# Two silus issued earlier on ScalarE, tile loads moved between steps, and the small tile's last product placed between two others

## The reference, cut to what matters

```
xn = layernorm(x)                                  # x: 4 x 1024 x 1024 fp32
s  = xn + attention over the batch axis (4 x 4 scores for each of 1024 positions)
Wg, Wu, Wd = NF4[codes] * scales of 64-blocks       # I = 2752, H = 1024
g  = silu( (silu(xn @ Wg.T) * (xn @ Wu.T)) @ Wd.T )
out = x + s * g
```

## Time and profile before

| what | value |
|---|---|
| median of 3 runs | 2513.22 us (2512.47 to 2515.49) |
| profiled execution, its own time | 2514.81 us |
| span in its profile | 2513.0 us |
| PE busy | 2414.7 us (96%), 11214 matmuls |
| DVE, ACT, POOL busy | 64%, 40%, 3% |
| mean granted TensorE clock | 0.985 |

### The profile page before, as it was taken

One profiled execution on the slowest core, in us unless ns is written; L12 is line 12 of the kernel. 1 busy time (PEld: TensorE's weight loads), 2 busy tenths in 40 slices (PEclk: granted clock), 3 DMA queues, 4 the chain that ended last, 5 costly groups with the idle time before them and its releaser, 6 DMA issues.

```text
span 2513.0 us, 30203 instructions
## 1 busy us (share of the span) xinstructions
PE 2414.7 (96%) x11214; PEld 1108.0 (44%) x11214; DVE 1604.2 (64%) x2751; ACT 1006.6 (40%) x1144; POOL 84.5 (3%) x72
## 2 busy tenths in 40 slices
PE   2889999999999989999999999999999999999999
PEld 1434444444444434444444444444444444444444
DVE  8888777668988857788877886656422432431431
ACT  8876777777778424444454521110000000000001
POOL 0000000000000000000000000000010011001011
PEclk7899999999999999999999999999999999999999
DMA  6856675657766795556655644229767766777764
GB/s 241 257 199 203 197 225 193 212 170 264 239 235 215 267 323 191 189 201 209 221 182 183 208 176 145 107 102 367 301 244 314 307 270 269 298 287 290 302 261 163
DMA packets 171854, 579.51 MB, mean 231 GB/s; under 512 B 17632, under 2 KB 42896, under 8 KB 153916
## 3 DMA queue, kind: packets, MB, share of 16 engines
q1 hardware_dynamic: 136716, 289.21, 33.9%
q10 hardware_dynamic: 34992, 288.37, 29.9%
HBM read 388.76 MB, written 188.75 MB: 230 GB/s over the span
## 4 chain that ended last, share of the span: by engine, by line
PE 87%; DVE 4%; issue 3%; DMA 3%; ACT 2%; SPq 0%; POOL 0%; ACTq 0%; POOLq 0%; DVEq 0%
PE ps L1764 55%; PE ps L1910 31%; DMA arena<-in_x 1%; ACT arena L760 1%; PE ps L1837 1%; PE ps L1721 1%; DMA arena<-xnsc 1%; DMA arena<-in_dn 1%; DVE arena L1291 0%; ACT arena L773 0%; DVE arena L1380 0%; DMA arena<-in_gu 0%; DVE arena L1223 0%; DVE arena L1433 0%; DVE arena L1312 0%
## 5 line engine op out<-in xcount | busy, mean ns | idle before, releaser
L1764 PE MATMUL ps<-arena 128*128 128x512 f16 x7152 | 1562.8, 381 | 34.5 <-ACT arena L966 11.3
L1764 PEld LDWEIGHTS ps<-arena 128*128 128x128 f16 x7152 | 701.7, 98 | 883.0 <-issue 19.4
L1910 PE MATMUL ps<-arena 128*128 128x512 f16 x3696 | 797.9, 379 | 0.3 <-issue 0.3
L760 ACT ACTIVATE arena<-arena,bias_t 128x2048 f32<-128x2048 f32 (+3 forms) x288 | 525.0, 1829 | 86.6 <-DMA arena<-in_dn 77.5
L1910 PEld LDWEIGHTS ps<-arena 128*128 128x128 f16 x3696 | 361.6, 98 | 436.6 <-issue 0.8
L1380 DVE TENSOR_TENSOR arena<-arena 128x512 f16<-128x512 f32 x364 | 243.1, 683 | 9.8 <-ACT arena L918 8.5
L1178 ACT ACTIVATE arena<-arena,e_d 128x512 f32<-128x512 f32 x48 | 34.6, 721 | 424.3 <-DVE arena L1686 219.4
L966 ACT ACTIVATE arena<-ps,gate_back 128x512 f32<-128x512 f32 x84 | 57.2, 681 | 301.7 <-PE ps L1764 301.5
L729 POOL TENSOR_TENSOR arena<-arena 128x512 f32<-128x512 f32 x64 | 82.5, 1297 | 2414.5 <-DMA arena<-in_xt 2106.1
L976 ACT ACTIVATE arena<-arena,gate_back 128x512 f32<-128x512 f32 x84 | 60.5, 720 | 179.1 <-DVE arena L1550 166.2
L1662 DVE SCALAR_TENSOR_TENSOR arena<-arena,sc 128x512 f32<-128x512 f32 x192 | 129.8, 743 | 0.0
(11 more groups left out here) (109 smaller groups left out, 1158.1 us busy)
## 6 DMA issues: line engine op xcount, KB each, us to landing
isc<-arena SPq DMA_DIRECT2D x308, 256.0 KB, 2.4
arena<-wdsc ACTq DMA_DIRECT2D x28, 2816.0 KB, 10.1
arena<-isc ACTq DMA_DIRECT2D x28, 2816.0 KB, 18.0
arena<-xnsc SPq DMA_DIRECT2D x48, 1024.0 KB, 8.5
wsc<-arena ACTq DMA_DIRECT2D x21, 1792.0 KB, 6.9
arena<-in_x SPq DMA_DIRECT2D x48, 512.0 KB, 6.0
arena<-in_gu ACTq DMA_DIRECT2D x43, 512.0 KB, 4.6
wdsc<-arena SPq DMA_DIRECT2D x77, 256.0 KB, 2.1
```

The costliest lines, as they stand in the source:

```text
L760: a_.activation(buf, src, ACT.Prelu, bias=bias_t[:, i:i + 1], scale=scale, alpha=alpha).then_inc(ramps, 1)
L1764: ins = t_.matmul(ps[:, bank, :], wreg[:, b, w, wa, k, :], xreg[:, j, o, k, xa, :], start=start and (k, wa, xa) == (0, 0, 0), stop=stop an ...
L1910: ins = t_.matmul(ps[:, bank, :], ring_w[b][:, k, wa, g, :], ring_i[b][:, k, xa, :], start=first and (k, wa, xa) == (0, 0, 0), stop=r not ...
```

## The change

1. `sil_a(s-1)` now stands in front of `w_high(2, 6)` in step 3.
2. In step 4 all ramps of tile 4 (`ramps_of(s, 0, 4)`) come behind `sil_a(3)` instead of partly in front, and `load_codes(4)` is issued in step 4, behind the high parts of tile 3, instead of at the end of step 3.
3. Behind a step of the rest, `halves` gives p1, p6 (of s), then p2 of the rest's step, then p7, p5. `second_half` of that step moves on DVE to a place between q and v of step s. This concerns steps 42, 44 and 86.
4. The rest's weights lie in slots 4 and 1 (`REST_W`) instead of 0 and 1: two 512-column high and low parts instead of one of 1024, a strided store, and other slots in the reload of the second half. At the turn slot 0 of tile 0 is loaded with slots 5 and 6 in step 41, and slot 4, which only p5 of step 44 reads, is loaded in step 43 with a semaphore of its own, `w4_in`.
5. The codes of tile 23 are loaded in step 42 instead of step 44.

```
-    if s > 2:
-        out += half(s - 1, SECOND, SECOND_REST)
-    return out
+    behind = half(s - 1, SECOND, SECOND_REST) if s > 2 else []
+    if out and STEPS[s - 1][1] == LAST:
+        return out[:2] + behind + out[2:]
+    return out + behind
...
+                for o, to in enumerate(REST_W):
+                    ins = a_.activation(wflat[:, b, to, 0, :], yb[2 * (LAST % 2)][:, 512 * o:512 * o + 512], ACT.Copy)
+                ins.then_inc(w_hi, 1)
...
                     act.wait_ge(prod, prod_at(39, "p3"))
-                    load_w(0, 4, 7)
+                    load_w(0, 0, 1)
+                    load_w(0, 5, 7)
...
-                if s in DOWN_AT and DOWN_AT[s][1] == 0 and DOWN_AT[s][0] + 1 < NDOWN:
+                if s in DOWN_AT and DOWN_AT[s][1] == 0 and 0 < DOWN_AT[s][0] < NDOWN - 1:
                     load_codes(NU + DOWN_AT[s][0] + 1)
+                if s == 42:
+                    load_codes(NU + 1)
...
+                if s == 4:
+                    load_codes(4)
...
-                if late:
+                if late and s != 4:
                     ramps_of(s, 2, 3)
+                if s > 2:
+                    sil_a(s - 1)
                 if s == 3:
                     w_high(2, 6)
-                if s > 2:
-                    sil_a(s - 1)
...
                     act.wait_ge(prod, prod_at(43, "r"))
-                    load_w(0, 0, 1)
+                    act.dma_start(wflat[:, wbuf(1, 0), 4, :, :], wsc[0, :, 4, :, :]).then_inc(w4_in, 16)
...
-                ramps_of(s, 3 if late else 2, 4)
+                ramps_of(s, 0 if s == 4 else 3 if late else 2, 4)
...
                 v_.tensor_tensor(q, ps[:, p6_bank(s), :], p1sb, ALU.add).then_inc(q_made, 1)
                 background(s, 1)
+                if s > 2 and STEPS[s - 1][1] == LAST:
+                    second_half(s - 1)
...
-                        pe.wait_ge(w_in[b][1 if w in (1, 2, 3) else 0], 32 * loads - (16 if u == LAST else 0))
+                        if u == 0 and w == REST_W[0]:
+                            pe.wait_ge(w4_in, 16)
+                        else:
+                            pe.wait_ge(w_in[b][1 if w in (1, 2, 3) else 0], 32 * loads - (16 if u == LAST else 0))
```

More of the change, by code:

```diff
@@ L42 @@
 FIRST_REST, SECOND_REST = ["p1", "r"], ["p2"]
+REST_W = [4, 1]
 DOWN_ORDER = ["p1", "p6", "p2", "p7", "p5", "p4", "p3"]
@@ L386, in build @@
         xb_in = [[sem(f"xb_in{j}{o}") for o in range(7)] for j in (0, 1)]
+        w4_in = sem("w4_in")
         prod = sem("prod")
@@ L778, in w_high_last @@
                 act.wait_ge(wst[LAST % 2], 16 * (LAST // 2))
+                act.wait_ge(prod, prod_at(step_of(0, LAST - 2, 1), "p5"))
                 act.wait_ge(prod, prod_at(step_of(0, LAST - 2, 1), "p2"))
-                a_.activation(wflat[:, b, 0:2, 0, :], yb[2 * (LAST % 2)].rearrange("p (o c) -> p o c", o=2), ACT.Copy).then_inc(w_hi, 1)
+                for o, to in enumerate(REST_W):
+                    ins = a_.activation(wflat[:, b, to, 0, :], yb[2 * (LAST % 2)][:, 512 * o:512 * o + 512], ACT.Copy)
+                ins.then_inc(w_hi, 1)
             def store_w(u):
@@ L785, in store_w @@
                 if u == LAST:
-                    act.dma_start(wsc[u, :, 0:2, :, :], wflat[:, b, 0:2, :, :]).then_inc(wst[u % 2], 16)
+                    act.dma_start(wsc[u, :, 1:5:3, :, :], wflat[:, b, 1:5:3, :, :]).then_inc(wst[u % 2], 16)
                 else:
@@ L1126, in _ @@
                     act.wait_ge(prod, prod_at(43, "r"))
-                    load_w(0, 0, 1)
+                    act.dma_start(wflat[:, wbuf(1, 0), 4, :, :], wsc[0, :, 4, :, :]).then_inc(w4_in, 16)
                 elif s == NSTEP + 40:
-                    load_w(LAST, 0, 1)
+                    load_w(LAST, 4, 5)
                     load_w(LAST, 1, 2)
@@ L1139, in _ @@
                     c_high(job, 3)
-                if 3 <= s < 40 and j:
+                if 4 <= s < 40 and j:
                     load_codes(u + 3)
@@ L1277, in w_item @@
                         dve.wait_ge(w_hi, w_base(u, 7, 1) + 1)
-                        v_.tensor_tensor(wflat[:, b, 0:2, 1, :], tg.rearrange("p (o c) -> p o c", o=2), wflat[:, b, 0:2, 0, :],
-                                         ALU.subtract).then_inc(w_lo, 1)
+                        for o, to in enumerate(REST_W):
+                            ins = v_.tensor_tensor(wflat[:, b, to, 1, :], tg[:, 512 * o:512 * o + 512], wflat[:, b, to, 0, :], ALU.subtract)
+                        ins.then_inc(w_lo, 1)
                     return
@@ L1641, in _ @@
                     background(s, 4)
-                if s > 2:
+                if s > 2 and (s == TOTAL or STEPS[s - 1][1] != LAST):
                     second_half(s - 1)
@@ L1859, in _ @@
                     if u == LAST and name == "r":
[L1860 to L1863, removed]
+                        for k, (w, o) in enumerate(zip(REST_W, (4, 2))):
+                            need(t, name, w, o)
+                            ins = product(t, bank, w, o, k == 0, k == 1)
                     else:
-                        w, o = (OPERAND[name],) * 2 if u != LAST else (0, 0) if name == "p1" else (1, 1)
+                        w, o = (OPERAND[name],) * 2 if u != LAST else (REST_W[0], 0) if name == "p1" else (REST_W[1], 1)
                         need(t, name, w, o)
```

## The result

| | before | after |
|---|---|---|
| median | 2514.26 us (4 runs, 2512.47 to 2515.49) | 2499.01 us (4 runs, 2497.79 to 2499.58) |
| ratio, 95% interval | | 0.9942 [0.9928, 0.9956] |
| profiled execution: own time, span | 2514.81, 2513.0 us | 2499.58, 2497.8 us |
| PE busy | 2414.7 us | 2409.7 us |

The account below looks back on a forecast made before the run. PE, busy 2414.7 of 2513.0 us, was taken as the bound, with its breaks. The terms 2.5 + 3.3 + 3.6 + 9.9 - 2.5 = 16.8 us took the median 2513.2 to 2496.4, stated as 2496.5, range 2490 to 2503.

Parts of the forecast that it names:

- Part 1: Silus of steps 3 and 4 on ACT moved forward: 2.5 us gained, bounds 0 to 5, limited by DVE.
- The item on the slow start near 276: PE behind 276.35: half of the 1.6 us of slow matmuls there was counted as saved.
- The last item: Ramps of tile 4: their codes, issued later, land after 9 us and cost 0.3 us.
- Rival (a): Steps 4 and 5: both silu breaks saved in full, 13.4 us instead of 2.5, time 2485.5 us; chance 0.07.
- rival (d): Step 3: late codes of tile 4 delay DVE, kernel slower; breaks even at 26 us of landing; chance 0.02.
- Part 2: Steps 43 and 87: PE's two 1.65 us waits for silu and multiplication go, 3.3 us.
- Part 3: Step 44: PE's 3.57 us break at 905.7, for the load of slot 0, goes, 3.6 us.
- Part 4: Turn, codes of tile 23 loaded earlier: PE's losses of 7.17 and 2.7 us go, 9.9 us.
- The deduction: Step 44: slot 1 of tile 0 lands 2 to 4 us late; 2.5 us off the gain, ends 0 and 6.
- The second path: Step 46, p7: scale rows of tile 22, about 14.6 us to land, may delay DVE; would overlap with slot 1's delay.
- Rival (b): Turn held by its transfers: costs over 6 of the 9.9 us, gain 6 to 10, 2503 to 2507 us; chance 0.14.
- rival (c): Slots 4 and 1 land so late that the turn takes as long; within 0.2%, 2508 us and up; chance 0.05.

Follow-up runs that it names:

- no_silus: The changed kernel with steps 3 and 4 on ACT put back as before; 2501.19 us, ratio 0.9954 to the kernel before.
- silus_only: The kernel before with only the silus, ramps and tile 4 codes of steps 3 and 4 moved; 2510.26 us, ratio 0.9988.
- codes4_old_place: The changed kernel with the codes of tile 4 asked for at the end of step 3 again; 2500.37 us, ratio 0.9952 to the kernel before.
- slots_only: The kernel before with only the rest's weights in slots 4 and 1 and slot 0 of tile 0 loaded in step 41; 2513.15 us, ratio 0.9994.
- slot1_first: The changed kernel with slot 1 of tile 0 asked for in front of two token operands; 2495.2 us, ratio 0.9924 to the kernel before.
- slot1_scales: As slot1_first, with the scale rows of tile 22 asked for in step 42 instead of 43; 2493.70 us, ratio 0.9915 to the kernel before.

## Why the prediction was right, point by point

**Part 1** was forecast as 2.5 us with 0 to 5. The mechanism is shown: PE stands for DVE's addition of p4 in steps 4 and 5 (forecast 3.1 and about 5; seen 2.22 and 2.92, and 3.10 and 4.12 in the run of part 1 alone), then for the silu of step 7, 3.8 us earlier than before. It measured 3.0 us alone and 3.0 in the change, by ratios that are uncertain by more than 2 us. At the mark of the short wait (354.03 before, 350.9 to 354.5 in the four other kernels without part 1 whose token tiles are all loaded; 347.7 to 349.8 in the six with it) the traces give some 4 us. The term was a little small: DVE could follow further than the 1.6 us that I read from its wait for PE at 203.02 (there is a second one, of 0.36 us at 192.66). The addition of p3 that waited there runs at 199.00 now, 4.0 us earlier. Part of it is that DVE's token tile came 1.9 us earlier (177.43 against 179.30); in the seven traces with the codes' old place and all token tiles it came at 178.5 to 179.8, in the four with the new place at 177.2 to 178.2, so the later codes, which I had down as a loss of 0.3, seem to have made room for it. The item on the slow start near 276 came out in full and not by half: the break there shrank from 2.47 to 0.79 us and nothing slow stands behind it, while the silu's break at 255.56 has one now (7.04 us for 24 matmuls against 5.35). Some of the 5.5 us at the mark is chance: `no_silus` has it 3.1 us earlier than the kernel before, and nothing that was changed between the two bears on PE before step 40. The last item, codes landing 9 us after they are asked for, was near: they are asked for at 168.62 and used at 176.86, and no cost of theirs can be told, as their old place shows. Rival (a), both breaks in full, and rival (d), the codes, are out by `silus_only` and `codes4_old_place`.

**Part 2**, 3.3 us: the waits are gone, and 3.8 us were measured alone (1.5 to 6.0). **Part 3**, 3.6 us: its break is gone in the change, but by these runs the term can hold only together with part 4: alone it gave 1.5 us by the ratio, which cannot be told from nothing. I added the terms without saying that. **Part 4**, 9.9 us: 9.6 by the ratio alone, 7.4 by the medians, and 8.2 in its trace, since 1.61 us of the break goes only with part 2. The four parts alone sum to 17.9 us by the ratios and the change gives 14.6; by the medians it is 15.3 and 15.3, so whether the parts simply add up stays open.

**The deduction** of 2.5 us, with 0 and 6 as ends, is the term that was mis-sized. The path was named rightly: slot 1 was the last of a row of loads, and it was 4.19 us late, with some 1.5 us lost to the lower level behind it (19.44 us for the first 83 matmuls against 83 x 0.216 = 17.9), 5.7 in all. The slow start was left out, though the same kind of loss stood in the other terms. The wait was 1.7 us longer than the 2.5. The times behind it were both wrong, and nearly cancelled. Slot 1 landed at 925.85, not at 929 to 931 (my own steps, 929.2 plus 3.6 less up to 3, give 929.8 to 932.8). PE came for it at 921.7, not at 927.6, a figure that left part 1's lead out. PE was earlier by its lead at the mark, and the landing moved with it, since that load waits for a product of PE (see `no_silus`). The bytes were counted at 359 GB/s, and while slot 1 was in flight the engines moved 6.17 MB in 18.6 us, 332 GB/s; I estimate 1.4 us from these two rates for that stretch. The second path, the scale rows, was named too, and is shown by `slot1_first` (2.74 us once the first path is free) and `slot1_scales` (both free, 6.8 us gained by the ratio).

**The sum.** The deduction was 3.2 us too small (5.7 against 2.5), and the whole forecast was 2.5 us too low, so the other terms together came to 0.7 us more than forecast. That they came so near is in part luck. By the two profiled executions the lead was 5.5 us at the mark (2.5 forecast, and partly chance), 9.4 at the turn (15.1 us of breaks and slow starts before, 5.7 after) and 1.65 in step 87; some 2.4 were lost near 1105 and 1326, where nothing was forecast.

**Rivals.** Rival (b), over 6 us lost at the turn, was only just missed, and its two halves do not fit: a loss of 6 us would give a gain of 13.3, 2499.9, and not the 6 to 10 us that it names, for which 9 or more must be lost; rival (c), no change because slots 4 and 1 both land late, is out, since slot 4 held nothing in the change.

**What stays open.** PE's waits for DVE near 1105 and 1326 took 3.1 us in the trace after and 2.3 in that of before, and a slow start of 1.7 us stands behind the first of them. In the other traces they sum to between 1.4 and 3.7 us, with and without the change; I take them for chance, and no run isolates them.

**The scale rows' time to landing.** The Trainium skill, DMA: Bandwidth & Descriptors, section Queues, rings and completion order, says that each DMA engine goes round the queues that have work, a packet at a time. From this the prediction had worked out, for an equal split in bytes, some 6 us for the scale rows on SP's queue; they landed after 17.1 (median of four). While they were asked for, 901.8 to 904.4, the two queues moved (packets, MB, share of the time of 16 engines; q10 is ACT's, q1 SP's):

```profile
q10 hardware_dynamic: 205, 0.60, 59.2%
q1 hardware_dynamic: 227, 0.42, 41.5%
```

The numbers of packets are near each other and the bytes are not, so this stretch agrees with packets taken in turn, and it was the step from packets to bytes that failed. SP's queue also carried stores that had been issued before the scale rows. How much of the 17.1 us was theirs no run shows.

## What to carry to other kernels

When waits follow one another in front of the same transfers, cost them as a chain. Taking away the first alone moved its time into the next in `slots_only`; in the changed kernel, where the load that the last wait hung on is moved up as well, both breaks are gone. Where a stage becomes shorter, sum up the bytes that must land in it and look at which load is asked for last; its place in the queue can be worth more than the moment at which it is asked for (`slot1_first`: 0.13 us earlier, 2 MB less in front, landed 5.5 us earlier). And where an in-order engine has a ramp or a high part in front of a silu that the bound engine waits for, moving it gains only up to what the next engine can follow.

## What the runs showed of the hardware that had not been expected

Whether a slow start follows a break does not go by the break's length alone. In step 4 PE stood for 3.10 us in `silus_only` and did the next 84 matmuls in 18.30 us, at a granted clock of 1.00 from the start; in the changed kernel it stood for 2.22 us and took 19.99, with 0.66 in the first 5 us; in `slots_only` it stood for 3.29 and took 21.18, with 0.50 in the first 5 us. In the kernel before, 3.57 us cost nothing more and 2.47 us cost 1.6. So in these traces breaks between 2 and 3.6 us cost their length and from 0 to 2.9 us more. This kernel has about five breaks of that kind, and that may be a good part of the spread between executions of one kernel (2509.3 to 2519.0 us in 15 executions of the kernel before). Only one execution of each kernel was traced, so this is not shown.
